# Entry, refill order and last loads of an expert stage: first group in two halves of two experts

## The reference, cut to its last layer

```python
h = xf @ W_router + b_router
Sm = jax.nn.softmax(h, axis=-1)
G_ek, idx_ek = jax.lax.top_k(Sm.T, k)             # 32 experts, k = 1250 // 32 = 39 tokens each
tokens = xf[idx_ek]
tok_g = tokens.reshape(NUM_GROUPS, GROUP_SIZE, k, H)                  # 8 groups of 4
up = jnp.einsum('gjkh,ghf->gjkf', tok_g, W_up) + b_up[:, None, None, :]   # D_FF = 1365
act = jax.nn.silu(up).reshape(E, k, D_FF)
Eout = jnp.einsum('ekf,efh->ekh', act, W_down) + b_down[:, None, :]
weighted = G_ek[..., None] * Eout
y = jnp.zeros((bs, H), dtype=x.dtype).at[idx_ek.reshape(-1)].add(weighted.reshape(-1, H))
```

## Time and profile before

| | us |
|---|---|
| median of 3 runs (lowest, highest) | 1669.67 (1669.47, 1671.43) |
| the profiled execution | 1668.56 |
| its span | 1666.7 |
| PE busy, whole span | 1468.8 |
| DVE busy, whole span | 682.8 |
| POOL busy, whole span | 460.1 |
| expert stage: first token turned to last matmul | 1365.78 to 1653.51 |

### The profile page before, as it was taken

The page is one execution under the profiler, slowest core; times in us unless marked ns, Lnnn a source line. Parts: engine busy times, 40 slices in busy tenths (PEclk is TensorE's granted clock), DMA queues, the critical chain, the costliest instruction groups (busy, mean ns, idle before and its releaser), DMA issues.

```text
span 1666.7 us, 18532 instructions
## 1 busy us (share of the span) xinstructions
PE 1468.8 (88%) x7115; PEld 978.5 (59%) x7115; DVE 682.8 (41%) x1240; ACT 371.1 (22%) x609; POOL 460.1 (28%) x447
## 2 busy tenths in 40 slices
PE   5999978999988489799999988999999719998986
PEld 3546745544557367577777734678866616654543
DVE  6422056789325714366666331424252461110100
ACT  2210003212020223244444405202152101100010
POOL 3100021004210301288788818102010022331111
PEclk9999998999989689899999999999999659999999
DMA  6000010005000021211111073003002925999995
GB/s 201 0 0 0 1 53 1 26 1 193 6 0 0 10 103 55 63 25 24 25 32 24 1 163 85 1 0 127 1 1 114 379 96 206 398 388 406 412 409 195
DMA packets 41611, 176.15 MB, mean 106 GB/s; under 512 B 6231, under 2 KB 6817, under 8 KB 39604
## 3 DMA queue, kind: packets, MB, share of 16 engines
q1 hardware_dynamic: 37499, 169.23, 28.1%
q0 software_dynamic: 3712, 5.40, 1.5%
q10 hardware_dynamic: 313, 0.35, 0.1%
HBM read 153.35 MB, written 19.05 MB: 103 GB/s over the span
## 4 chain that ended last, share of the span: by engine, by line
PE 75%; DVE 8%; DMA 6%; SPq 4%; POOL 3%; issue 2%; ACT 2%; POOLq 0%; DVEq 0%; ACTq 0%
PE psum L996 9%; PE psum L987 6%; PE psum L1018 6%; PE psum L1251 5%; PE psum L1472 5%; PE psum L1153 5%; PE psum L1452 4%; PE psum L1010 4%; PE psum L1239 3%; SPq L422 3%; PE psum L1210 3%; PE psum L1330 3%; DMA arena<-in_w_down 2%; PE psum L1240 2%; PE psum L1142 2%
## 5 line engine op out<-in xcount | busy, mean ns | idle before, releaser
L676 POOL TENSOR_TENSOR arena<-arena 125x420 f32<-125x420 f32 x192 | 178.5, 930 | 27.3 <-ACT arena L901 0.7
L1472 PE MATMUL psum<-arena 128*39 128x512 f32 (+1 forms) x704 | 158.5, 607 | 12.5 <-DMA arena<-in_w_down 9.6
L1766 DVE TENSOR_REDUCE neg_max<-psum 125x1 fp32r<-125x1250 f32 x80 | 116.7, 1459 | 113.0 <-PE psum L1210 113.0
L901 ACT ACTIVATE arena<-psum 125x420 f32<-125x420 f32 x240 | 107.8, 521 | 130.7 <-PE psum L1240 130.7
L1472 PEld LDWEIGHTS psum<-arena 128*39 128x39 f32 (+1 forms) x704 | 51.5, 117 | 113.5 <-issue 108.7
L1018 PE MATMUL psum<-arena 128*125 128x512 f32 (+3 forms) x344 | 108.3, 475 | 4.1 <-issue 2.4
L987 PE MATMUL psum<-arena 128*128 128x512 f32 (+1 forms) x288 | 105.1, 527 | 1.3 <-ACT arena L782 0.7
L1251 PE MATMUL psum<-arena 125*64 125x210 f32 x960 | 102.7, 349 | 0.0
L758 POOL DMA_INDIRECT out_x<-arena,idx x32 | 44.8, 1400 | 206.8 <-DMA out_x<-arena,idx 119.9
L1452 PEld LDWEIGHTS psum<-arena 128*128 128x128 f32 (+1 forms) x704 | 95.6, 191 | 8.2 <-issue 5.7
L1452 PE MATMUL psum<-arena 128*128 128x156 f32 (+1 forms) x704 | 97.7, 302 | 2.3 <-DVE arena L1993 1.6
(11 more groups left out here) (358 smaller groups left out, 2355.6 us busy)
## 6 DMA issues: line engine op xcount, KB each, us to landing
arena<-in_w_down SPq DMA_DIRECT2D x96, 768.0 KB, 19.8
arena<-in_w_up SPq DMA_DIRECT2D x32, 682.5 KB, 17.5
arena<-in_w_down SPq DMA_DIRECT2D x32, 512.0 KB
a_spill<-arena SPq DMA_DIRECT2D x1, 5468.8 KB
adj<-a_spill SPq DMA_DIRECT2D x1, 5468.8 KB
bc<-k_dram SPq DMA_DIRECT2D x16, 312.5 KB, 4.5
gw<-in_gw SPq DMA_DIRECT2D x2, 2048.0 KB, 8.7
arena<-in_wkqv SPq DMA_DIRECT2D x1, 3072.0 KB, 20.1
```

What stands on the lines that cost most here:

```text
L676: pool.tensor_tensor(SUMS[rnd % 2], SUMS[rnd % 2], PT[s % P_RING], ALU.add).then_inc(sum_added, 1)
L1472: ins = pe.matmul(o[64 * j:64 * j + CAP, :], ACTT[g % 2][0:w, f, at:at + CAP], DN[e % 5][0:w, f], start=f == 0, stop=f == FT - 1)
L1766: dve.tensor_reduce(neg_max[:, k:k + 1], max_bank[:, 0:N], AX.X, ALU.max, negate=True).then_inc(max_ready, 1)
```

## The change

Five edits, all in the expert stage (one wait on constants is merged too: `ones_dk_ready` is dropped and `const_ready` is used in its place, which frees a semaphore for `down_half`):

1. Up products of group 0 are computed by pairs: two tokens turned, up products of pair 0 with 78 moving columns, the next two tokens turned, down products of pair 0, up products of pair 1, four tokens of group 1 turned, down products of pair 1. There are four more wide blocks (`COL`), numbered by `up_blocks` and `up_done`. ScalarE applies silu to 78 columns at a time there.
2. Later tokens are turned one group ahead instead of two. Gathers, DVE's copies and `moe_rows` follow that order; POOL issues three groups of gathers at the start, and the fourth between the scatters of pair 0 and pair 1.
3. Down buffers are refilled by halves: PE counts `down_half` when strips 0 to 5 of a pair are done, and the first half of the next expert's weights waits for that, the second half for the whole pair.
4. The SP order at the entry is experts 5, 6, up 2 and 3 of group 1, expert 7. The last two experts load their first halves, then their second halves.
5. DVE waits for `xf_stored` after top-k instead of before it.

```diff
+def up_blocks(g):
+
+    if g == 0:
+        return [(COL["up"] + 4 * p + q, 2 * CAP * p, 2 * CAP, q) for p in range(2) for q in range(4)]
+    return [(COL["up"] + 4 * (g + 1) + q, 0, 4 * CAP, q) for q in range(4)]
+
+
+def up_done(g):
+    return COL["up"] + 4 * (g + 2)
...
-            def load_down(e):
-                if e >= 5:
+            def load_down_half(e, i):
+                if e >= 5 and i == 0:
+                    sp.wait_ge(down_half, (e - 5) // 2 + 1)
+                elif e >= 5:
                     sp.wait_ge(rows_full, PAIR_ROW[(e - 5) // 2] + 1)
...
-            for g in range(1, EXPERT_GROUPS):
-                for c in range(2 if g == 1 else 0, 4):
+            load_down(5)
+            load_down(6)
+            load_up(1, 2)
+            load_up(1, 3)
+            load_down(7)
+            for g in range(2, EXPERT_GROUPS):
+                for c in range(4):
                     load_up(g, c)
-                for e in range(1 if g == 1 else 0, 4):
-                    load_down(4 * g + e)
+                for e in range(4 * g, min(4 * g + 4, EXPERTS - 2)):
+                    load_down(e)
+            for i in range(2):
+                for e in range(EXPERTS - 2, EXPERTS):
+                    load_down_half(e, i)
...
-            for g in range(4):
+            for g in range(3):
                 gather(g)
             for g in range(EXPERT_GROUPS):
-                if g + 4 < EXPERT_GROUPS:
-                    gather(g + 4)
                 for i in range(4):
+                    if i == (2 if g == 0 else 0) and g + 3 < EXPERT_GROUPS:
+                        gather(g + 3)
...
+            turn_tokens(0, 0, 2)
+            wait_up(0)
+            pe.wait_ge(rows_free, TOKEN_ROW[1] + 1)
+            up_products(0, up_blocks(0)[0:4])
+            turn_tokens(0, 2, 4)
+            pe.wait_ge(cols_free, COL["up"] + 4)
+            down_products(0, 0)
+            pe.wait_ge(rows_free, TOKEN_ROW[3] + 1)
+            up_products(0, up_blocks(0)[4:8])
+            turn_tokens(1, 0, 4)
+            pe.wait_ge(cols_free, up_done(0))
+            down_products(0, 1)
+            for g in range(1, EXPERT_GROUPS):
+                pe.wait_ge(rows_free, TOKEN_ROW[4 * g + 3] + 1)
+                wait_up(g)
+                up_products(g, up_blocks(g))
+                if g + 1 < EXPERT_GROUPS:
+                    turn_tokens(g + 1, 0, 4)
+                pe.wait_ge(cols_free, up_done(g))
                 for p in range(2):
...
-            dve.wait_ge(xf_stored, 32)
             cur, other = SMT, SMT2
...
+            dve.wait_ge(xf_stored, 32)
+            drain_tokens(0, 0, 2)
+            drain_tokens(0, 2, 4)
+            gate_pair(0)
+            drain_tokens(1, 0, 4)
+            gate_pair(1)
```

More of the change, by code:

```diff
@@ L131, in moe_rows @@
 def moe_rows():
[L133 to L136, removed]
+    order = [("tokens", e) for e in range(PER_GROUP)] + [("out", 0)]
+    order += [("tokens", PER_GROUP + i) for i in range(PER_GROUP)] + [("out", 1)]
+    for g in range(1, EXPERT_GROUPS):
+        if g + 1 < EXPERT_GROUPS:
+            order += [("tokens", PER_GROUP * (g + 1) + i) for i in range(PER_GROUP)]
         order += [("out", 2 * g), ("out", 2 * g + 1)]
@@ L952, in _ @@
             for g in range(EXPERT_GROUPS):
-                for q in range(4):
-                    i = COL["up"] + 4 * g + q
+                for i, at, n, q in up_blocks(g):
                     act.wait_ge(cols_full, i + 1)
@@ L1426, in _, with turn_tokens @@
             ins.then_inc(rows_full, 1)
-            def turn_tokens(g):
-                for i in range(PER_GROUP):
+            def turn_tokens(g, lo, hi):
+                for i in range(lo, hi):
                     p, at = i // 2, 64 * (i % 2)
@@ L1437, in turn_tokens, with up_products, down_products, wait_up @@
                     ins.then_inc(rows_full, 1)
[L1439 to L1443, removed]
+            def up_products(g, blocks):
+                for n, at, width, q in blocks:
+                    o = open_col(n)
+                    for f in range(3 * q, min(3 * q + 3, FT)):
+                        w = 128 if f < FT - 1 else FREST
+                        for c in range(C):
+                            ins = pe.matmul(o[0:w, (f - 3 * q) * 512:(f - 3 * q) * 512 + width],
+                                            UPQ[(4 * g + c) % 6][:, f * 128:f * 128 + w], TKT[g % 2][:, c, at:at + width],
+                                            start=c == 0, stop=c == C - 1)
+                    ins.then_inc(cols_full, 1)
+            def down_products(g, p):
+                o = open_row(PAIR_ROW[2 * g + p])
+                for f in range(FT):
+                    if f in (0, DOWN_HALF):
+                        half = "dn_end" if f else "dn"
+                        for j in range(2):
+                            e = 4 * g + 2 * p + j
+                            pe.wait_ge(loads[f"{half}{e % 5}"], 32 * (e // 5 + 1))
+                    w = 128 if f < FT - 1 else FREST + 1
+                    for j in range(2):
+                        e = 4 * g + 2 * p + j
+                        at = (2 * p + j) * CAP
+                        ins = pe.matmul(o[64 * j:64 * j + CAP, :], ACTT[g % 2][0:w, f, at:at + CAP],
+                                        DN[e % 5][0:w, f], start=f == 0, stop=f == FT - 1)
+                    if f == DOWN_HALF - 1:
+                        ins.then_inc(down_half, 1)
+                ins.then_inc(rows_full, 1)
+            def wait_up(g):
                 for c in range(C):
@@ L1446, in _ @@
                     pe.wait_ge(loads[f"up{n % 6}"], 16 * (n // 6 + 1))
[L1447 to L1455, removed]
@@ L1972, in _, with drain_tokens @@
             dve.wait_ge(rows_free, ROW["topk_t"] + 1)
-            def drain_tokens(g):
-                for i in range(PER_GROUP):
+            def drain_tokens(g, lo, hi):
+                for i in range(lo, hi):
                     o = filled(TOKEN_ROW[4 * g + i])
```

71 lines of the change are left out of this document (30 added, 41 removed).

## The result

| | us |
|---|---|
| changed kernel, median of 13 runs (lowest, highest) | 1675.21 (1672.23, 1679.07) |
| kernel before, same chip, median of 13 runs | 1668.67 (1664.48, 1672.18) |
| ratio, 95% interval | 1.0041 (1.0028 to 1.0053) |
| profiled execution of the changed kernel, its span | 1679.07, 1677.3 |

The change costs 6.5 us between the medians, where 6.7 us of gain were predicted. The timeline of PE in the changed kernel (start, length, line, operation, count, idle time ahead of it and releaser) answers the earlier trace rows: L1461 are turned tokens, L1472 up products, L1490 down products.

The account below looks back on a forecast made before the run. The DMA weight stream was taken to set the end of groups 3 to 7; 5.2 us from the stream and 1.8 from the tail, less 0.3, gave -6.7: median 1663.0 (profiled 1661.9), range over all 1659.5 to 1669.2.

Parts of the forecast that it names:

- Part 1: Before the gathers: top-k no longer waits for the stored tokens, so all that follows starts 1.74 us earlier; called certain.
- Part 2: PE's entry: two turned tokens suffice instead of eight, so the first up product starts at 1365.4 instead of 1373.84.
- Part 3: Group 0's up products by pairs: pair 0 11.8 us, pair 1 9.5, together 21.3 against 14.28, 7.0 dearer.
- Part 4: PE's chain through group 0: group 1's up products end at 1420.0 against 1420.8, PE alone gaining 0.8 us.
- Part 5: Weight queue: stream 5.2 us ahead at group 2's third up part, data from 1421.3, no running dry afterwards.
- Part 6: Last pairs, interleaved halves: last matmul at 1646.5 against 1653.51, gain 7.0 us, 5.2 from stream and 1.8 from tail.
- A: Pair 0's up products: clock stays at 1.2 GHz throughout, 18.0 us, 6.2 more; total 1668.9 us; chance 0.12.
- B: Group 0's up products: a 78-column pass is no shorter than the 0.135 us of 156 columns; total 1667.6; chance 0.09.
- C: Pair 1's up products: narrow passes pull the clock down again there too, price 11.3 us; total 1674.0; chance 0.05.
- D: Before pair 13: stream's lead holds, clock doesn't fall; last matmul 1645.0, total 1661.5; within the forecast, together 0.74.
- Slower: Whole kernel: measured slower than before, where measurement tells about 0.2%, 3.3 us; chance 0.05.

Follow-up runs that it names:

- e1: Changed kernel, but pair 0's up products move their 78 columns twice, 156 a pass, the second copy unused; ratio 0.9990 to the kernel before.
- e13: Kernel before with three edits alone: wait for stored tokens behind top-k, refill by halves, last halves interleaved; ratio 0.9967 to the kernel before.
- e3: Changed kernel plus five unused 512-column products on TensorE round top-k's turn; ratio 1.0032 to the kernel before.
- e4: Kernel before plus five unused 512-column products on TensorE round top-k's turn; ratio 0.9996 to the kernel before.
- e9: Changed kernel with group 0's up products whole, four tokens turned first, and group 1's two up parts ahead of expert 5; ratio 0.9965 to the kernel before.

## Why the prediction was wrong

By its own steps, times from the gates where the executions differ:

- **Part 1** held in the trace: no idle ahead of top-k.
- **Part 2** held: the first up product at 6.46, predicted 1365.4 - 1359.2 = 6.2.
- **Part 3 failed**, and it is the step that turned the sign. I took "4.8 us again" of low clock from the 156-column products and put it under 78-column ones. The term was 11.8 and measured 18.47. The size of a pass was right at either level: 9.76 / 88 = 0.111 at full clock (taken 0.108), 18.47 / 88 = 0.210 at the lower (taken 0.205). What was wrong was to carry over a time to rise from one shape to another, though the earlier trace rows already showed 32-column passes at 0.50 with PE busy throughout; the clock didn't rise within pair 0's products at all. e1 shows it by the shape alone. Even for 156 columns 4.8 was one draw of 3.2 to 5.2.
- **Part 4** missed what follows from it: the down products of pair 0 were costed at full clock (9.55) and began at the lower one, 12.22; ScalarE's wait with the turns was 1.04 and not 0.6. Sum of the misses: 6.67 + 2.67 + 0.44, and 0.3 at the entry, 0.2 and 0.1 for pair 1, about 10.4. Group 1's up products were predicted at 60.8 and ended at 71.1: 10.3.
- **Part 5** was right as a mechanism: the queue stands before group 2's third up part, the data flow 1.1 us behind the end of group 1's up products (1.3 taken), and there is a hole in front of it, 103 GB/s in 1432 to 1436, worth 3 us where 5 were predicted. PE's delay passed through it whole: 72.26, where 1421.3 - 1359.2 = 62.1 was predicted. As foretold, there is no later hole, and PE's first wait for weights falls in group 4. What failed is that the sum has no term for the moved gathers: I looked for who waits for POOL and not at what its DMAs take from a full stream, 2.0 to 2.3 us for four gathers. My account of a group's bytes had the term in sight, 35.6 us "before the small gathers and scatters take their part", and gave it no number.
- **Part 6**: the interleaving gave what was said, 1.67 against 1.8 after against before. It gave it in another way: pair 15 did wait for expert 31 (0.53 and 0.90), as I had said it wouldn't, because with a late stream the end is set by its last half; without interleaving the wait is 3.21 and the clock falls.
- **Rivals.** A is what happened, and was priced 1668.9, against 1675.2. Its pass was right (18.0 against 18.47). It missed the low clock under the down products behind it (2.67), 1.5 in small terms of the entry (10.35 in all, where A had 6.2) and the longer stream (2.8): 1668.9 + 4.15 + 2.8 = 1675.9, and the baseline was 1.0 lower in this measurement, 1674.9. The rule of the Trainium skill that I cited beside it (TensorE: Matmul & The Clock Gate, "HAM oscillation — how this bites in real kernels") is about short bursts of products with waits between them, each of which starts at the reduced rate. It isn't what these runs show: the row of 18.47 us has no wait inside it, and e1 had the same waits ahead of it (5.28 and 0.86 against 5.33 and 0.85) and took 13.49. B and C didn't occur (9.76 for pair 1), D's condition neither: pair 13 waited 1.98 and ran at the lower clock, 11.35 us.
- **The chances.** 0.12 for A was too low, with the 32-column row for it and only a 64-column row at full clock, which came with the clock already up, against it. Slower held 0.05, since A was priced 6 us short and so counted as no change.

## What to carry to other kernels

Before splitting a product into narrower ones at a place where the engine has been idle, ask at which clock they will run: take the price of a pass from rows at the lower level too, and price the products behind it at that level as well, unless a row of that shape shows the clock rising. When the stream is the limit, count every small transfer that a reordering moves into it, and check each edit of a bundle alone: here the low clock under the split cost some 8 us (e1) and the gather order 2, while the moved wait, the halves and the interleaved last loads together gained without them (e13, 0.9967).

## What the runs showed of the hardware

- The same 88 passes of 78 columns took 18.47 us where the clock was low when they began, and 9.76 where it was up. PE and its weight loads counted as busy throughout in both. From the same low start the clock rose 3.3 us into passes of 156 columns in e1 (3.2 to 5.2 over eleven kernels), and 5.2 us into the down products of 512 columns of the changed kernel (0.67 over 1392 to 1396: 2.6 of 4 us at one half, so 1394.6 against 1389.47). What it is in a narrow pass that keeps the level isn't shown.
- The clock rose under unused work (e3: 1.00 in 1362 to 1368), but it was gone after waits of 2.49 and 0.85 us with eight small turns between them; in e4 it fell among turns and waits alone.
- Four gathers of 39 rows of 2 KB, 0.32 MB together, cost a full stream 2.0 to 2.3 us, the time of 0.8 to 0.9 MB at 399 GB/s.
- ScalarE's table load for the first silu came 2.9 and 4.4 us later against the first up product in e9 and e13 than in the kernel before, for no reason that the profile names; PE then waited 2.29 and 0.68 us for it, and in e13 had stopped for another 2.31 us by itself.
